# A four-layer graph network on one core: frames of counts that hold one tile each, the first block's panels moved to the end, block ends counted in groups, low one-hots against a PSUM iota, and a wait moved into a loop

## The chip, the core and the metric

The kernel runs on one core of a Trainium2 chip. The metric is the device time of one execution, in microseconds (us); before the change it is 7200.89 us, the median of three runs (7191.73 to 7232.2). One execution was recorded by the profiler.

## The reference

There are 12,500 nodes with 64 features and 200,000 edges sorted by their destination `dst`; each edge has 32 attributes and one of 16 types. Four layers follow one another, each of the form `x = x + layer(relu(layernorm(x)))`:

```python
x = x + L0(h)   # segment_sum((h @ weight[type])[src], dst) + bias + h @ loop_weight
x = x + L1(h)   # concat(h, segment_sum(h[src], dst)) @ W.T + b
x = x + L2(h)   # mean over dst of mlp(concat(h[src], h[dst], attr)) + h @ Wn + bn
x = x + L3(h)   # concat(h, segment_sum(concat(h[src], attr) @ W1 + b1, dst)) @ W2 + b2
```

`src` is drawn evenly over all nodes. `dst` is drawn as 12500 u squared, so that the first nodes have many edges each and the last ones few.

## The kernel before

**Units of work.** 128 edges are a tile, 4 tiles (512 edges) a group; there are 392 groups. 128 nodes are a window (98 of them), 7 windows a block of nodes (14 blocks). The kernel runs setup, `first_nodes` (a table of projected features), and then `layer_phase` for layers 0 to 3. Groups 0 to 383 of layer 0 and groups 272 to 383 of layers 1 and 3 are written out one by one (the static part). Behind them `run` does the last 8 groups and the last block in a loop with lengths read from a table (the dynamic part). Layer 2 is a loop throughout.

**A group, the gathered way.** GpSimd gathers the rows of the 512 sources by 4 indirect DMAs (line 1128) into one of 8 `msg` buffers. VectorE compares the edges' destinations with `window_iota` into `sel` (line 1514), TensorE multiplies and sums them (line 1811), and VectorE adds the result to `acc`, the sums of all nodes (line 1531).

**Counts.** The sums over the sources of the first 272 groups need no gather in layers 1 and 3. Layer 0 builds a table for them: for a frame (a few neighbouring destinations) it counts how many edges go from each of the 12,544 sources to each destination of the frame. A frame's width is the most destinations that its tiles may span. `PANEL_SHAPES` lists (groups, tiles to a frame, width); before, the first 192 groups have frames of two tiles, the other 80 frames of one tile, 704 frames and 20 panels in all. For a pair of tiles VectorE makes one-hots of the source's low 7 bits (`low_hot`, line 1559) and of its high part with the destination (`frame_hot`, line 1570). TensorE multiplies them unit by unit into two PSUM tensors (`count_pair`, line 1835), ScalarE casts each unit into `frames` (`evacuate`, line 1348), SyncE stores a group's frames to `counts` (line 1220), and VectorE checks one window of them (`certify`, line 1587). This work is spread over the 384 steps of layer 0 by `pairs_before`, one step to a gathered group, in proportion to width + 3. In a step TensorE does `sum_up` and then the step's pairs; ScalarE places the next group's attributes and then evacuates; VectorE selects the next group, certifies, makes the one-hots and adds the sums.

**Panels.** In layers 1 and 3 a panel is a run of groups whose frames fill up to 512 columns. TensorE multiplies the 98 windows of node features with the panel's counts (line 1851), in 4 pieces of 25, 25, 25 and 23 matmuls; SyncE loads the pieces into a ring of 3. That is one step to a piece, 80 steps. When a panel is complete, ScalarE copies its low half (line 1449), VectorE adds the halves (`combine`, line 1594), and in the next four steps `add_frames` adds each frame to its place in `acc`, one instruction to a frame (line 1613):

```python
if (t - begin) % LOADED == 0:
    count = min(LOADED, end - t)
    _, bases = nc.values_load_multi_w_load_instructions(
        frame_base[0:1, bass.ds(frames_before[k] + t, count)], engines=[DVE_ENGINE], ...
to = acc[0:D, bass.ds(bases[(t - begin) % LOADED], fw)]
```

The destinations' first columns are thus read into registers, up to 16 at a time, by line 1607. `panel_sums` and `panel_ps` have two buffers each. The gathered groups 272 to 383 are spread over the same steps.

**Blocks.** When all sums of a block are there, the five parts of `node_part` finish its nodes, one part to a step: ScalarE copies `acc` to `stage` (line 1364), TensorE multiplies it (line 1872), VectorE adds to `xs` (line 1629), normalises, and so on. `BLOCK_ENDS` gives, in steps of 8 groups, the group by which a block is complete; `part_at` is made from it at build time, on all engines alike. In layers 1 and 3 four blocks come behind the last panel: 5, 12, 6 and 7. VectorE then copies the iota back (line 1746), waits for the last static block's store (line 1748), and goes into `run`.

`ordered` is 1 where the inputs keep the bounds of the static part, and 0 sends everything to the dynamic part in many passes.

## Time and profile before

| what | value |
|---|---|
| median of three runs | 7200.89 us (7191.73 to 7232.2) |
| the profiled execution's own time | 7163.53 us |
| its span | 7161.7 us |
| mean granted TensorE clock | 0.743 of full speed |
| setup and `first_nodes` | 0 to 240 us |
| layer 0 | 240 to 2717 us |
| layer 1 | 2717 to 3638 us |
| layer 2 | 3638 to 6342 us |
| layer 3 | 6342 to 7162 us |

PE is TensorE's matmuls, PEld its weight loads, DVE VectorE, ACT ScalarE, POOL GpSimd, SPq SyncE's DMA issues. Reads into registers are not counted as busy: on VectorE they are seen as idle time with the releaser "issue", and in the chain of waits as "DVEq".

### The profile page before, as it was taken

To read this page: it belongs to the slowest core of one execution; us is meant where nothing else is said; L and a number is where in the kernel's file an instruction comes from. 1 tells how busy PE (TensorE), PEld (TensorE's weight loads), DVE (VectorE), ACT (ScalarE), POOL (GpSimd) and SP (SyncE) were. 2 spreads that over 40 slices of the span, in tenths; PEclk is the share of its full clock that TensorE was granted. 3 is DMA by queue.
4 is the path that set the end of the run, shared out by engine and by line. 5 is a ranking of instruction groups with operands and counts; after the bars stand their busy time and mean duration, and the time that the engine had idled before them with its cause. 6 is when DMAs were issued, how large, how long until landed. Compare 5 with 4: busy or idle time off the path is not lost. (4 is left out here: it accounts for less than half of the span.)

```text
span 7161.7 us, 86379 instructions
## 1 busy us (share of the span) xinstructions
PE 4714.0 (66%) x24800; PEld 3020.3 (42%) x24815; DVE 2438.5 (34%) x6392; ACT 2060.6 (29%) x3761; POOL 3998.2 (56%) x4125
## 2 busy tenths in 40 slices
PE   6565665666676656888646666666666666668885
PEld 3343443333333332344435554455545555533433
DVE  6443343333443333434222222222222222234232
ACT  5333333333566550010112222222222222210000
POOL 0466666666666555655246665555555555546653
PEclk8656567677666677888667887777777777778886
DMA  5433333332333335655222222222222222245562
GB/s 212 148 70 71 73 77 77 78 80 76 103 105 110 99 98 178 210 199 199 66 54 63 64 64 60 61 62 60 59 59 58 60 59 58 60 144 203 191 206 74
DMA packets 626790, 724.54 MB, mean 101 GB/s; under 512 B 235557, under 2 KB 526858, under 8 KB 607084
## 3 DMA queue, kind: packets, MB, share of 16 engines
q1 hardware_dynamic: 427578, 506.86, 21.5%
q0 software_dynamic: 130976, 185.66, 11.7%
q10 hardware_dynamic: 67986, 28.96, 1.5%
q8 instruction: 123, 2.02, 0.1%
q14 instruction: 127, 1.04, 0.0%
HBM read 518.59 MB, written 201.58 MB: 101 GB/s over the span
## 5 line engine op out<-in xcount | busy, mean ns | idle before, releaser
L1117 POOL DMA_INDIRECT layer_msg<-snd_table,layer_idx x1565 | 1480.3, 946 | 1305.7 <-DMA rel_table<-first_rows 442.8
L1128 POOL DMA_INDIRECT layer_msg<-rel_table,idx_rel x1536 | 1556.7, 1013 | 840.0 <-issue 420.9
L1811 PE MATMUL layer_sum_ps<-layer_sel,layer_msg 128*128 128x128 f32 (+14 forms) x8192 | 1139.7, 292 | 986.3 <-issue 445.8
L1835 PE MATMUL layer_unit_ps<-layer_frame_hot,layer_low_hot 128*128 128x350 bf16 (+9 forms) x3792 | 1111.5, 440 | 758.9 <-ACT layer_frames L1348 425.6
L1811 PEld LDWEIGHTS layer_sum_ps<-layer_sel,layer_msg 128*97 128x97 f32 (+2 forms) x8192 | 1069.4, 209 | 1161.1 <-issue 638.6
L1348 ACT CAST layer_frames<-layer_unit_ps 128x700 fp8e4<-128x700 f32 (+9 forms) x1268 | 953.1, 785 | 1341.0 <-remote 539.0
L1128 POOL DMA_INDIRECT layer_msg<-h_table,idx_src x896 | 849.9, 949 | 658.5 <-issue 238.5
L1851 PE MATMUL layer_panel_ps<-layer_piece,layer_pairs 128*128 128x504 fp8e4 (+9 forms) x3920 | 953.8, 399 | 124.6 <-issue 84.5
L1835 PEld LDWEIGHTS layer_unit_ps<-layer_frame_hot,layer_low_hot 128*128 128x128 bf16 x3792 | 395.3, 124 | 1310.4 <-issue 614.0
L1522 DVE TENSOR_TENSOR layer_msg<-layer_pre_ps,layer_msg 128x512 f32<-128x512 f32 x392 | 270.3, 690 | 1128.6 <-remote 696.0
L1851 PEld LDWEIGHTS layer_panel_ps<-layer_piece,layer_pairs 128*128 128x128 f16 x3920 | 391.2, 103 | 622.1 <-issue 253.5
L1531 DVE TENSOR_TENSOR acc<-acc,layer_sum_ps 64x64 f32 (+15 forms) x632 | 130.3, 206 | 1418.2 <-DMA rel_table<-first_rows 649.3
L1794 PEld LDWEIGHTS layer_pre_ps<-layer_rcv,layer_sel_t 128*128 128x128 f32 x3144 | 489.0, 221 | 266.9 <-issue 266.9
L1318 ACT COPY layer_attr_t<-layer_flip_ps 128x128 f32<-128x128 f32 x394 | 104.9, 266 | 1677.8 <-remote 1178.0
L1570 DVE TENSOR_SCALAR layer_frame_hot<-count_iota,frame_key 128x588 bf16<-128x588 f16 (+9 forms) x1088 | 560.7, 563 | 58.3 <-remote 35.3
L1791 PE MATMUL layer_pre_ps<-w_edge,layer_attr_t 128*128 128x512 f32 x786 | 531.1, 766 | 0.0
L1794 PE MATMUL layer_pre_ps<-layer_rcv,layer_sel_t 128*128 128x128 f32 x3144 | 472.8, 300 | 0.0
L1613 DVE SCALAR_TENSOR_TENSOR acc<-layer_panel_sums,ordered,acc 64x14 f32 (+9 forms) x1408 | 319.6, 227 | 444.2 <-issue 259.0
L1514 DVE TENSOR_TENSOR layer_sel_bf<-rel_dst,layer_window_iota 128x512 bf16<-128x512 f32 x395 | 269.9, 684 | 385.3 <-DMA rel_table<-first_rows 172.9
L1449 ACT COPY layer_low_sums<-layer_panel_ps 64x504 f32<-64x504 f32 (+9 forms) x40 | 22.0, 551 | 951.0 <-PE layer_panel_ps L1851 366.8
L1514 DVE TENSOR_TENSOR layer_sel<-rel_dst,layer_window_iota 128x256 f16<-128x256 f32 (+15 forms) x632 | 229.5, 370 | 128.6 <-issue 57.0
L1328 ACT ACTIVATE layer_msg<-layer_msg 128x512 f32<-128x512 f32 x392 | 251.1, 641 | 50.8 <-DVE layer_msg L1522 36.9
(236 smaller groups left out, 3780.6 us busy)
## 6 DMA issues: line engine op xcount, KB each, us to landing
layer_piece<-counts SPq DMA_DIRECT2D x48, 1575.0 KB
layer_attr<-in_edge_attr_dram SPq DMA_DIRECT2D x790, 64.0 KB
rel_table<-first_rows SPq DMA_DIRECT2D x98, 512.0 KB, 2.7
layer_piece<-counts SPq DMA_DIRECT2D x24, 1500.0 KB
layer_piece<-counts SPq DMA_DIRECT2D x16, 1593.8 KB
layer_rcv<-rcv_table SPq DMA_DIRECT2D x396, 64.0 KB
layer_msg<-snd_table,layer_idx POOLq DMA_INDIRECT x1565
layer_piece<-counts SPq DMA_DIRECT2D x16, 1543.8 KB
```

Of the source, the lines that this page charges most:

```text
L1117: nc.gpsimd.indirect_dma_start(msg[g][:, u, 0:2 * D if dense else width], None, of, bass.IndirectOffsetOnAxis(ap=idx_slot[g][:, u:u + 1], ...
L1128: nc.gpsimd.indirect_dma_start(msg[g][:, u, 0:2 * D if dense else width], None, of, bass.IndirectOffsetOnAxis(ap=idx[:, at:at + 1], axis=0 ...
L1348: nc.scalar.copy(part, of, saturate=False).then_inc(evacuated, 1)
L1514: nc.vector.tensor_tensor(to[:, :, 0:span], rel.unsqueeze(2).to_broadcast([P, TILES, span]), window_iota[:, 0:span].unsqueeze(1).to_broadc ...
L1522: nc.vector.tensor_tensor(rows_of, pre_ps[g % 2][:, :], rows_of, ALU.add).then_inc(pre_added, 1)
L1570: last = nc.vector.tensor_scalar(frame_hot[j][:, v, 0:HI * fw], count_iota[:, 0:HI * fw], frame_key[:, tile:tile + 1], None, ALU.is_equal)
L1613: nc.vector.scalar_tensor_tensor(out=to, in0=panel_sums[k % 2][:, t * fw:(t + 1) * fw], scalar=ordered[0:D, 0:1], in1=to, op0=ALU.mult, op ...
L1791: nc.tensor.matmul(pre_ps[g % 2][:, :], attr_t[g % 2][:, :], w_edge[:, :], start=True, stop=False)
L1794: last = nc.tensor.matmul(pre_ps[g % 2][:, u * H:(u + 1) * H], sel_t[g % 2][:, u * P:(u + 1) * P], rcv[j][:, :], start=False, stop=u == TI ...
L1811: last = nc.tensor.matmul(sum_ps[g % 2][0:sums, 0:span], msg[g][:, u, c0:c1], sel[j][:, u, 0:span], start=n_part == 0, stop=n_part == len( ...
L1835: last = nc.tensor.matmul(unit_ps[unit % 2][:, half * 512:half * 512 + cols], low_hot[k % HOT][:, 2 * (r % 2) + v, :], frame_hot[j][:, v, ...
L1851: last = nc.tensor.matmul(panel_ps[k % 2][:, 0:count * fw].rearrange("p (t f) -> p t f", t=count), pairs[:, w // KW, (w % KW) * 2 * D:(w % ...
```

## The change

`PANEL_SHAPES` has 22 panels, all with one tile to a frame: 1088 frames where there were 704, with widths 4 to 17. `SEQUENCE` gives the order in which layers 1 and 3 take the panels: 3 to 21, then 0, 1 and 2 (78 groups, all within block 0). Those three have 128, 100 and 84 frames; the first two of the new order have 64 each. There are 88 steps in place of 80. Block 0 is now finished last, and three blocks come behind the last panel's combining: 7, 12 and 0. `BLOCK_ENDS` is counted in single groups, so that a block of layer 0 can begin up to 7 steps earlier; the last static block of layer 0 begins at step 379 and not behind the last group. `low_hot` is made against `window_iota`, which lies in PSUM, and not against `iota` in SBUF. The wait for `stored` moves from ahead of `run` into `nodes`, behind the 8 groups of the loop. `FRAME_MAX` falls from 20 to 17, the most frames' columns that a one-hot buffer must hold.

```diff
-PANEL_SHAPES = ((42, 2, 6), (28, 2, 9), (22, 2, 11), (19, 2, 13), (18, 2, 14), (15, 2, 17), (15, 2, 17),
-                (13, 2, 19), (12, 2, 20), (8, 2, 20), (9, 1, 13), (9, 1, 13), (9, 1, 14), (9, 1, 14), (9, 1, 14),
-                (8, 1, 15), (8, 1, 15), (8, 1, 16), (6, 1, 17), (5, 1, 17))
+PANEL_SHAPES = ((32, 1, 4), (25, 1, 5), (21, 1, 6), (16, 1, 8), (16, 1, 8), (14, 1, 9), (13, 1, 9),
+                (12, 1, 10), (11, 1, 11), (11, 1, 11), (10, 1, 12), (10, 1, 12), (9, 1, 13), (9, 1, 13),
+                (9, 1, 14), (9, 1, 14), (9, 1, 14), (8, 1, 15), (8, 1, 15), (8, 1, 16), (7, 1, 17),
+                (5, 1, 17))
...
-FRAME_MAX = 20
+FRAME_MAX = 17
...
-BLOCK_ENDS = (14, 19, 23, 27, 30, 33, 35, 38, 40, 42, 44, 46, 48, 49)
+BLOCK_ENDS = (107, 151, 184, 212, 237, 259, 279, 298, 316, 333, 349, 364, 379)
...
+LATE = 3
+SEQUENCE = list(range(LATE, len(PANELS))) + list(range(LATE))
+LATE_GROUPS = PANELS[LATE][0]
...
-            first_step[b] = (BLOCK_ENDS[b] - FIRST) * PER
+            first_step[b] = BLOCK_ENDS[b] - FIRST * PER
...
-                ends = min(BLOCK_ENDS[b] * PER, DENSE_1)
-                ready = PIECES * (2 + min(k for k, panel in enumerate(PANELS) if panel[0] + panel[1] >= ends))
+                ends = min(BLOCK_ENDS[b], DENSE_1)
+                needed = [k for k, n in enumerate(SEQUENCE) if PANELS[n][0] < ends and (b == 0 or n >= LATE)]
+                ready = PIECES * (2 + max(needed))
...
-            for _, ng, tiles, _, _ in PANELS:
+            for n in SEQUENCE:
+                _, ng, tiles, _, _ = PANELS[n]
...
-                            iota[:, :].unsqueeze(1).to_broadcast([P, TILES, P]), ALU.is_equal)
+                            window_iota.unsqueeze(1).to_broadcast([P, TILES, P]), ALU.is_equal)
...
 def add_frames(k, s):
-                    _, _, _, fw, _ = PANELS[k]
+                    g0, _, tiles, fw, _ = PANELS[SEQUENCE[k]]
+                    at = g0 * TILES // tiles if tiles == 2 else g0 * TILES - DOUBLE_1 * TILES // 2
...
-                                frame_base[0:1, bass.ds(frames_before[k] + t, count)], engines=[DVE_ENGINE],
+                                frame_base[0:1, bass.ds(at + t, count)], engines=[DVE_ENGINE],
...
                 def nodes(b, m):
+                    dve.wait_ge(stored, 16 * stores * (static_blocks + 1))
...
-                    dve.wait_ge(stored, 16 * stores * (static_blocks + 1))
                 run(dve, DVE_ENGINE, edges, nodes, next_window)
```

The other lines of the diff put `PANELS[SEQUENCE[k]]` for `PANELS[k]` on each engine, and let setup's bounds say that the first 78 groups lie in block 0.

## Rows read from the trace of the kernel before

**Rows 1.** Windows by stage: us, busy (instructions) of PE, PEld, DVE, ACT, POOL; clock; DMA.

```profile
240.00:2717.00 2477.00, 1547.47 (x7420) 912.54 (x7420) 991.03 (x2597) 1062.17 (x1730) 1589.47 (x1571) 0.65 0.33 84
2717.00:3638.00 921.00, 677.47 (x3606) 356.85 (x3606) 335.59 (x1152) 78.06 (x174) 454.59 (x479) 0.81 0.50 166
...
6342.00:7162.00 820.00, 608.93 (x3172) 292.35 (x3172) 260.12 (x981) 36.84 (x48) 452.68 (x479) 0.81 0.53 175
```

**Rows 2.** The page's costliest groups: count, busy us, mean ns, idle before.

```profile
L1128 POOL DMA_INDIRECT layer_msg<-rel_table,idx_rel x1536 | 1556.7, 1013 | 840.0 <-issue 420.9
...
L1835 PE MATMUL layer_unit_ps<-layer_frame_hot,layer_low_hot 128*128 128x350 bf16 (+9 forms) x3792 | 1111.5, 440 | 758.9 <-ACT layer_frames L1348 425.6
...
L1128 POOL DMA_INDIRECT layer_msg<-h_table,idx_src x896 | 849.9, 949 | 658.5 <-issue 238.5
```

**Rows 3.** Windows in layer 0; POOL's instructions there are the gathers of line 1128.

```profile
400.00:1700.00 1300.00, 806.74 (x4026) 504.35 (x4027) 510.59 (x1416) 471.63 (x776) 881.10 (x875) 0.65 0.32 75
1800.00:2600.00 800.00, 544.29 (x2423) 282.68 (x2423) 322.76 (x785) 479.38 (x768) 488.20 (x476) 0.66 0.37 105
```

**Rows 4.** Groups by shape, layer 0.

```profile
L1559 DVE TENSOR_TENSOR layer_low_hot<-low_key,iota 128x512 bf16<-128x512 f32 x272 | 186.1, 684 | 0.0
...
L1348 ACT CAST layer_frames<-layer_unit_ps 128x1000 fp8e4<-128x1000 f32 x80 | 78.1, 993 | 139.0 <-PE layer_unit_ps L1835 70.8 <-remote 55.5 <-DVE layer_cert L1587 6.6
...
L1570 DVE TENSOR_SCALAR layer_frame_hot<-count_iota,frame_key 128x588 bf16<-128x588 f16 x168 | 55.5, 378 | 43.8 <-remote 27.6 <-PE layer_unit_ps L1835 9.1 <-issue 6.8
L1570 DVE TENSOR_SCALAR layer_frame_hot<-count_iota,frame_key 128x1960 bf16<-128x1960 f16 x80 | 54.9, 728 | 0.0
...
L1348 ACT CAST layer_frames<-layer_unit_ps 128x550 fp8e4<-128x550 f32 x88 | 53.8, 619 | 112.2 <-remote 54.9 <-PE layer_unit_ps L1835 39.5 <-issue 9.2
...
L1514 DVE TENSOR_TENSOR layer_sel<-rel_dst,layer_window_iota 128x512 f32<-128x512 f32 x8 | 5.5, 683 | 7.4 <-issue 4.9 <-PE layer_sum_ps L1811 2.5
```

**Rows 5.** Waits in 1800 to 2600 us: who for whom, us, times, longest.

```profile
PEld layer_unit_ps L1835 <- ACT layer_frames L1348: 287.8, 292, 5.5
...
POOL layer_msg L1128 <- PE layer_sum_ps L1811: 148.5, 42, 9.0
```

**Rows 6.** Timeline of VectorE in layer 3's first panel: start, us; idle before in brackets.

```profile
6436.90 5.57 DVE L1613 SCALAR_TENSOR_TENSOR acc<-layer_panel_sums,ordered,acc 64x6 f32 x16 [3.80 <-issue]
6443.60 1.61 DVE L1613 SCALAR_TENSOR_TENSOR acc<-layer_panel_sums,ordered,acc 64x6 f32 x5 [1.13 <-issue]
```

**Rows 7.** Windows cut where a panel's sums are combined (line 1594), layers 1 and 3.

```profile
2777.00:2829.70 52.70, 37.63 (x171) 14.36 (x169) 21.60 (x96) 0.58 (x1) 31.84 (x34) 0.84 0.57 195
2829.70:2862.70 33.00, 28.04 (x146) 11.87 (x146) 15.85 (x71) 0.56 (x1) 19.43 (x21) 0.90 0.57 198
2862.70:2890.70 28.00, 26.06 (x138) 11.14 (x138) 12.84 (x56) 0.57 (x1) 18.41 (x20) 0.94 0.68 247
2890.70:3481.60 590.90, 476.33 (x2696) 248.52 (x2696) 227.43 (x812) 51.76 (x115) 336.19 (x353) 0.88 0.56 189
...
6519.00:7080.60 561.60, 446.73 (x2422) 215.75 (x2420) 179.44 (x705) 25.34 (x34) 337.42 (x357) 0.86 0.56 188
```

**Rows 8.** Chain of waits, 6400 to 6480 us, by line.

```profile
by line: DVE acc L1613 31.5%; DVEq L1607 24.8%; issue 19.2%; PE layer_panel_ps L1851 11.4%; DVEq L1613 6.4%; DVE layer_sel L1514 2.3%; DVE acc L1531 1.8%; ACT layer_low_sums L1449 0.7%; DVEq L1076 0.6%; PE layer_sum_ps L1811 0.5%; another c
```

**Rows 9.** Timeline of VectorE, end of layer 1.

```profile
3518.04 0.68 DVE L1629 SCALAR_TENSOR_TENSOR xs<-layer_post_ps,ordered,xs 128x448 f32<-128x448 f32 x1
...
3541.53 0.68 DVE L1629 SCALAR_TENSOR_TENSOR xs<-layer_post_ps,ordered,xs 128x448 f32<-128x448 f32 x1
...
3577.46 0.29 DVE L1746 COPY layer_window_iota<-iota 128x128 f32<-128x128 f32 x1 [0.22 <-DVE xs L1629]
3592.31 0.69 DVE L1514 TENSOR_TENSOR layer_sel<-rel_dst,layer_window_iota 128x512 f16<-128x512 f32 x1 [14.55 <-issue]
```

**Rows 10.** Line 1746, the end of each static part, and who waited.

```profile
L1746 DVE COPY layer_window_iota<-iota x3: 294/295/296, 2671.9 to 7129.5; 128x128 f32<-128x128 f32 x3
...
  DVE layer_sel L1514: 4.6, 1
```

More of the change, by code:

```diff
@@ L389, in _ @@
                 link(nc.vector.tensor_scalar(double[:, :], group_of[:, :], float(DOUBLE_1), None, ALU.is_lt))
-                count_from(lowest, BLOCK_ENDS[0] * PER, 1.0)
-                for end in BLOCK_ENDS[1:NB - 1]:
-                    count_from(lowest, end * PER)
+                count_from(lowest, BLOCK_ENDS[0], 1.0)
+                for end in BLOCK_ENDS[1:]:
+                    count_from(lowest, end)
                 link(nc.vector.tensor_scalar(lowest[:, :], lowest[:, :], float(BLK), None, ALU.mult))
                 count_from(outside, DENSE_1, float(N))
-                link(nc.vector.tensor_scalar(highest[:, :], outside[:, :], float(8 * BLK - P), None, ALU.add))
+                link(nc.vector.tensor_scalar(width_step[:, :], group_of[:, :], float(LATE_GROUPS),
+                                             float(BLK - 8 * BLK), ALU.is_lt, ALU.mult))
+                link(nc.vector.scalar_tensor_tensor(out=highest[:, :], in0=outside[:, :],
+                                                    scalar=float(8 * BLK - P), in1=width_step[:, :], op0=ALU.add,
+                                                    op1=ALU.add))
                 link(nc.vector.memset(any_bad[:, :], 0.0))
@@ L874, in layer_phase @@
             if b <= 7:
-                ends = min(BLOCK_ENDS[b] * PER, DENSE_1)
-                ready = PIECES * (2 + min(k for k, panel in enumerate(PANELS) if panel[0] + panel[1] >= ends))
-            if BLOCK_ENDS[b] * PER > DENSE_1:
+                ends = min(BLOCK_ENDS[b], DENSE_1)
+                needed = [k for k, n in enumerate(SEQUENCE) if PANELS[n][0] < ends and (b == 0 or n >= LATE)]
+                ready = PIECES * (2 + max(needed))
+            if BLOCK_ENDS[b] > DENSE_1:
                 ready = max(ready, 1 + min(z for z in range(STEPS)
-                                           if DENSE_1 + groups_by[z] >= BLOCK_ENDS[b] * PER))
+                                           if DENSE_1 + groups_by[z] >= BLOCK_ENDS[b]))
             first_step[b] = ready
@@ L1224, in load_piece @@
                 def load_piece(s):
-                    _, ng, tiles, fw, at = PANELS[s // PIECES]
+                    _, ng, tiles, fw, at = PANELS[SEQUENCE[s // PIECES]]
                     w = ng * TILES // tiles * PIECE * fw
@@ L1443, in _ @@
                         if z % PIECES == 0 and 0 <= k < len(PANELS):
-                            _, ng, tiles, fw, _ = PANELS[k]
+                            _, ng, tiles, fw, _ = PANELS[SEQUENCE[k]]
                             cols = ng * TILES // tiles * fw
@@ L1589, in combine @@
                 def combine(k):
-                    _, ng, tiles, fw, _ = PANELS[k]
+                    _, ng, tiles, fw, _ = PANELS[SEQUENCE[k]]
                     cols = ng * TILES // tiles * fw
@@ L1841, in multiply_piece @@
                 def multiply_piece(k, s):
-                    _, ng, tiles, fw, _ = PANELS[k]
+                    _, ng, tiles, fw, _ = PANELS[SEQUENCE[k]]
                     count = ng * TILES // tiles
```

## The prediction

> **What bounds the kernel now.** I first cut the span by stage [rows 1]. No engine fills a stage: in layer 0 GpSimd is busy 1589 of 2477 us and TensorE 1547, in layer 1 TensorE 677 of 921. So I looked at each stage for the wait that ends last. Layer 2 holds no line of the diff, and setup only a few small ones; they stand at no change.
>
> Layer 0 goes at the pace of its steps, one gathered group (4 gathers) to a step. Two windows [rows 3] give it: 875 gathers in 1300 us are 218.75 groups, 5.94 us each, while the frames hold two tiles; 476 in 800 us are 119 groups, 6.72 us each, while they hold one. A gather takes 1013 ns and some 0.27 to 0.30 us of issue lie behind it (840 us of idle for 1536 gathers, half of it "issue" [rows 2]; the rest comes with blocks and waits), so gathers alone would allow about 5.2 us. They don't set the pace: GpSimd itself waits for TensorE to free a `msg` buffer, 42 times for 148.5 us, and TensorE's count matmuls wait for ScalarE's casts, 287.8 us out of 800 [rows 5]. The loop between TensorE and ScalarE sets it, in the late part above all: there ScalarE is busy 479.4/119 = 4.03 us a step and TensorE 544.3/119 = 4.57, against 2.16 and 3.69 in the early one [rows 3].
>
> The static parts of layers 1 and 3 go panel by panel. The windows between combines [rows 7] show two kinds. The first three panels' frames (84, 56, 44) are added in 52.7, 33.0 and 28.0 us. The next 16 panels take 590.9/16 = 36.9 us each in layer 1, blocks and gathered groups included, and 561.6/16 = 35.1 in layer 3. In the first, VectorE is "busy" 21.6 of 52.7 us and yet is the bound: the chain over such a stretch lies on line 1613 with 31.5% and on the register reads of line 1607 with 24.8%, TensorE's panels with 11.4% [rows 8]. The timeline [rows 6] gives a price to a frame: 16 adds in 5.57 us behind 3.80 us of reads, 5 in 1.61 behind 1.13, so 21 frames in 12.11 us, 0.577 us a frame. 84 frames: 48.4 us, and the window is 52.7, 4.3 us more. Thus D(n) = 0.577 n + 4.3 us; for 56 it says 36.6 where 33.0 was measured, so it may be 10% high there. It exceeds TensorE's 36.9 us from about 56 frames on.
>
> **Dense layers.** Frames rise from 704 to 1088 and panels from 20 to 22, panel matmuls from 1960 to 2156. VectorE, alone, would pay 384 x 0.577 = 222 us a layer, but the panels with few frames hide theirs behind TensorE. In the new order (64, 64, 56, 52 and on down to 20, then 128, 100, 84) the first two and the last three are bound by VectorE.
>
> Layer 1 before: first combine 2777.0 to line 1746 at 3577.5 [rows 7, 9], 800.5 us. After: 2 x D(64) = 82.4. Then 17 panels: the 16 of before, 590.9, and one more like the third window, 28.0, in which TensorE is busy 26.06; but the 112 gathered groups now go over 88 steps, not 80, so 17 panels hold 86.5 and not 16 + 1 windows' 89.6 + 5.6, 8.7 fewer. That window has 146 matmuls, 98 of them the panel's; the other 48 for 5.6 groups at 26.06/146 us make 1.5 us a group, minus 13. So 606. Then D(128) + D(100) = 78.2 + 62.0 = 140.2. In these late panels block 6 begins as well; a block behind the adds costs 23.5 us here, by 3518.04 to 3541.53 [rows 9], and in a stretch bound by VectorE I count it in full. Behind the last combine come the 84 frames, 52.7, with block 7 beside them, and then blocks 12 and 0, 47.0. Sum 952, +151.
>
> Layer 3: 1746 at 7129.5 [rows 10], first combine three windows like those of layer 1 before 6519.0, at 6405: 724.5 us. After: 82.4 + (561.6 + 26.5 - 13 = 575) + 140.2 + one block + 52.7 + two blocks. The stretch behind the last combine was 48.9 us for four blocks, 12.2 each; so 12.2 and 24.4. Sum 887, +162. Together +313 us. The orders of block 0 and of the table cost no more by themselves. The 12.5% more bytes of counts (118.8 to 133.7 MB by the shapes, stored once and loaded twice) run at 189 to 247 GB/s and a DMA share of 0.56 to 0.68 [rows 7], under matmuls or adds that take longer; with that cover gone, 14.9 MB at 247 GB/s would be 60 us a layer.
>
> Bounds of the dense term. Below: if the reads ahead of the adds overlapped more, a frame would cost near 0.35 us, the adds' own cadence (5.57/16), and the two layers would lose about 100 us, from two more panels and 128 frames at 45 us. Above: block parts and gathered sums interleave badly with the long adds; 360 us.
>
> **Layer 0, the counts.** By the shapes, units go from 1268 to 1580, matmuls from 3792 to 3160 and their columns from 1,427,600 to 1,065,600; ScalarE's cast columns rise from 947,200 to 1,065,600. Casts take 993 ns for 1000 columns and 619 ns for 550 [rows 4], so 0.165 us + 0.83 ns a column: 312 x 0.165 + 118,400 x 0.00083 = 150 us more. VectorE's `frame_hot` goes by 728 ns for 1960 and 378 for 588 [rows 4], 0.255 ns a column, of which 354,760 go: 90 us less, not on the path. The three memsets where the width drops go with them, under 4 us.
>
> What this does depends on how it is spread. Pairs go to steps by width + 3. Before, the 80 one-tile groups have 1407 of 4385 weights, the last 123 of 384 steps; after, the same widths have 1427 of 3480, 157 steps. A late step so has 22% less of counts: ScalarE's 4.03 us falls by 0.85. As the wait is for ScalarE, the 6.72 should fall by nearly that; I take 5.95. In the early 227 steps TensorE's count columns go from 960,800/261 = 3680 a step to 2610, ScalarE's from 1840 to 2610 (+0.64 us and a unit's fixed part, to some 2.9 us). TensorE's 3.69 falls to about 2.9. The two become equal; I take 5.70, a small gain. Before 261 x 5.94 + 123 x 6.72 = 2377; after 227 x 5.70 + 157 x 5.95 = 2228: -149. The last static block no longer stands behind the last group: a block costs some 12 us, as in the four behind the last combine of layer 3 (48.9 us). Earlier blocks merely move. In all -160. Bounds: 0 (the longer ScalarE takes all) and -365 (5.2 us a step, less the blocks' own delays). TensorE's granted clock is 0.65 of full speed in both windows [rows 3], 0.84 to 0.94 in the dense ones [rows 7], a share of time between its levels of 1.2 and 2.4 GHz. I leave it there; were it 0.60 after, TensorE's 2.9 to 3.6 us a step would be 0.25 to 0.3 longer, up to 110 us over 384 steps, within the bound of 0.
>
> **Low one-hots from PSUM.** The 272 instructions took 684 ns with both inputs in SBUF; the comparison of the same shape that reads `window_iota` in PSUM took 683 [rows 4]. Nothing; the bounds are +-0.1 us x 272, hidden on VectorE either way.
>
> The gathers take 1013 ns in layer 0 and 949 without counts beside them [rows 2], 64 ns x 1536 = 98 us of GpSimd. That could be the one-hots' doing; since GpSimd waits for TensorE, none of it reaches the end in my sum. The Trainium skill ("SBUF — State Buffer", section "Who interferes with whom") has VectorE and GpSimd share one pair of SBUF ports under an exclusive lock, and a VectorE instruction with an input in PSUM doesn't take it; by that rule 272 x 0.68 us of lock go, up to 98 us of gathers. The trace shows the excess, not its cause; my sum would be the same by either, and the rule only lowers the floor of the first rival.
>
> **The moved wait.** Behind line 1746 the next selection in layer 1 begins after 14.55 us, in layer 0 after 4.6 [rows 9, 10]: the last static block's store. Moved behind the loop's groups it is over when reached, -10 us; layer 3's block ends in little to store, layer 0 has its own wait small: -1.5. Queued behind the old place were VectorE's selections and all that follows; behind the new one only the last block's parts. -11.5, bounds 0 and -20.
>
> **Sum.** 7163.5 (own time of the profiled execution) + 313 - 160 - 11.5 = 7305, a ratio of 1.0197. The median of the three runs is 7200.9, 0.5% above that execution; times the ratio, 7343, say 7340 us.
>
> **Rivals.**
> (A) Layer 0 drops to the gathers' floor. For it: GpSimd's issue and gathers need only 5.2 us, TensorE loses 25% of its columns, and a waiting chain can release more than its busy time. Against: ScalarE's work rises, and blocks stall the step anyway. It decides if a step falls below 5.3 us. -340 in place of -160: 7125, 7162 on the median. This is the one that ends on the other side.
> (B) The frames are cheap or hidden. For it: 56 frames took 33.0, less than D says, and a short read was 1.13 us for 5. Against: the chain [rows 8]. It decides if a 128-frame panel takes under 50 us. +100 in place of +313: 7092, 7129 on the median.
> (C) Layer 0 gains nothing: ScalarE, already the releaser [rows 5], has 150 us more. 7465, 7503 on the median.
> (D) The change does not do what it says: a tile wider than its new bound sets `ordered` to 0 and costs many passes, far above all here. The tile spans of dst as 12500 u squared lie within the widths, so 1%.
>
> **How the numbers follow.** Mine 0.58, A 0.14, B 0.11, C 0.16, D 0.01. Mine has its own range, 7240 to 7430, from +313 by -60 and +50 and -160 by -50 and +60. To leave out no more than 2 in 10 the range takes in A and half of C: 7140 to 7490. A measurement of this kernel tells 0.5% from no change, 7165 to 7237. Faster: B, most of A, 0.16. Same: the edge of mine and the rest of A, 0.11. Slower: 0.73.
>
> **What would show it.** In the profile after: line 1613 x2176 and a larger share of line 1607 in the chain; the last two distances between combines near 78 and 62 us with TensorE busy under half; 17 near 35.6; steps of layer 0 near 5.7 and 5.95 us, casts near 1210 us busy; `low_hot` still 684 ns; the selection behind 1746 within 5 us in layer 1. The prediction is wrong if the adds of a step run without their reads in between (B), if layer 0's step reaches 5.2 (A), or if its late step stays at 6.7 (C).

## The result and the profile after

The changed kernel took 7290.77 us, the median of four runs (7273.74 to 7305.39), against 7196.31 us (7176.05 to 7232.2) for the kernel before on the same chip: a ratio of 1.0142, interval 1.0116 to 1.0169. It is slower, as forecast, by 94 us where 139 were forecast.

The experiments ran later, on chips numbered 2 (e1 to e8), 9 (e9 to e11) and 15 (e12). The kernel before takes 5720 to 5729 us on each of the three, so they are taken together here and called the second chip. The same change costs more there: 5915.09 us, 1.0341 (1.0324 to 1.0359). The first measurement has no chip number. "The first chip" is a name for it; whether it was a slower chip or a slower time of one isn't known. All ratios are to the kernel before, measured beside the run on the same chip, and all traces of experiments are of the second.

The page after, first chip, its costliest groups; they answer to [rows 2]:

```profile
L1141 POOL DMA_INDIRECT layer_msg<-rel_table,idx_rel x1536 | 1497.2, 975 | 895.0 <-issue 409.1
...
L1849 PE MATMUL layer_unit_ps<-layer_frame_hot,layer_low_hot 128*128 128x300 bf16 (+10 forms) x3160 | 1015.0, 452 | 791.7 <-ACT layer_frames L1361 488.6
L1361 ACT CAST layer_frames<-layer_unit_ps 128x600 fp8e4<-128x600 f32 (+10 forms) x1580 | 1082.2, 724 | 1206.9 <-PE layer_unit_ps L1849 568.6
...
L1627 DVE SCALAR_TENSOR_TENSOR acc<-layer_panel_sums,ordered,acc 64x8 f32 (+12 forms) x2176 | 485.2, 223 | 626.3 <-issue 341.3
```

The count matmuls lost a quarter of their columns and only 9% of their time: 1111.5 to 1015.0 us, 440 to 452 ns each although they are narrower. (The nanoseconds are a mean over instructions that overlap one another.) Windows of layer 0 show a lower clock beside it (all of the layer, then the two stretches of [rows 3]; the clock is the third number from the end):

```profile
240.00:2660.00 2420.00, 1496.24 (x6687) 857.56 (x6687) 877.55 (x2551) 1186.80 (x2035) 1523.38 (x1563) 0.56 0.36 91
400.00:1700.00 1300.00, 819.47 (x3575) 470.45 (x3576) 463.75 (x1485) 638.39 (x1101) 829.30 (x853) 0.52 0.36 91
1800.00:2600.00 800.00, 507.33 (x2269) 283.07 (x2269) 285.66 (x711) 416.65 (x672) 491.12 (x501) 0.63 0.35 96
```

The granted clock, a mean between the levels of 1.2 and 2.4 GHz, fell from 0.65 of full speed [rows 1] to 0.56. Most of the fall is early: 0.65 to 0.52 in the first stretch, 0.66 to 0.63 in the second. A step takes 1300/(853/4) = 6.10 us in the first stretch, 5.94 before, and 800/(501/4) = 6.39 in the second, 6.72 before.

A combine is VectorE's adding of a panel's two halves (line 1594 before, 1607 after), and its start marks a finished panel. The copy is that of the iota at the end of a static part (line 1746 before, 1761 after). The windows of the dense layers 1 and 3, cut at combines (first two panels of layer 1, the next 17, the two before the last combine, the rest to the copy; then the last three of layer 3), answer to [rows 7]:

```profile
2767.70:2833.40 65.70, 56.29 (x282) 23.05 (x281) 34.24 (x151) 1.16 (x2) 40.56 (x43) 0.90 0.67 234
2833.40:3420.00 586.60, 497.79 (x2751) 251.54 (x2750) 256.26 (x957) 48.95 (x108) 326.98 (x344) 0.90 0.62 207
3420.00:3484.70 64.70, 48.71 (x216) 22.31 (x214) 37.21 (x154) 5.37 (x12) 25.89 (x29) 0.84 0.53 180
3484.70:3544.40 59.70, 33.70 (x150) 18.76 (x150) 24.95 (x112) 4.59 (x10) 16.83 (x18) 0.70 0.20 39
3544.40:3637.50 93.10, 33.79 (x122) 25.80 (x123) 37.02 (x126) 10.86 (x25) 0.00 (x0) 0.54 0.07 20
7074.10:7132.40 58.30, 43.71 (x189) 17.91 (x187) 31.85 (x140) 2.42 (x3) 26.27 (x28) 0.83 0.55 188
7132.40:7189.40 57.00, 30.37 (x123) 13.80 (x123) 24.41 (x111) 2.32 (x3) 15.23 (x17) 0.68 0.13 12
7189.40:7255.60 66.20, 13.21 (x36) 8.47 (x36) 21.08 (x91) 3.69 (x4) 0.00 (x0) 0.50 0.03 7
```

The span of each trace can be cut at five instructions of VectorE, the three copies and the first combine of layers 1 and 3:

| stretch, us | first chip, before | after | forecast | second chip, before (e10) | after (e9) |
|---|---|---|---|---|---|
| start to copy in layer 0 | 2671.9 | 2660.0 (-11.9) | -160 | 2305.3 | 2214.9 (-90.4) |
| to first combine, layer 1 | 105.1 | 107.7 (+2.6) | 0 | 84.3 | 102.2 (+17.9) |
| to copy, layer 1 | 800.4 | 869.8 (+69.4) | +151 | 639.3 | 776.2 (+136.9) |
| to first combine, layer 3 | 2827.5 | 2819.2 (-8.3) | -10 | 2099.7 | 2084.4 (-15.3) |
| to copy, layer 3 | 724.5 | 798.9 (+74.4) | +162 | 570.2 | 704.1 (+133.9) |
| to the end | 32.2 | 31.4 (-0.8) | -1.5 | 31.7 | 30.4 (-1.3) |
| span | 7161.7 | 7287.0 (+125.3) | +141 | 5730.5 | 5912.2 (+181.7) |

On the first chip each column is one execution. The one before took 7163.5 us, 33 less than its median, and the one after 7288.8, 2 less than its own. So the parts add up to 125 us where the medians differ by 94, and a part of 12 us can't be told from nothing there.

Two terms of the forecast were too large, with opposite signs: the dense layers cost +144 and not +313, layer 0 gave 12 and not 160.

### The profile page after: what moved, and what is told of

It is laid out like the page before. It is cut to its first block and busy times, and to the rows that moved or that the text cites. A ratio compares the mean times of both kernels' runs of the same rounds, so it can differ in the third digit from the quotient of the medians.

```text
span 7287.0 us, 87827 instructions
## 1 busy us (share of the span) xinstructions
PE 4777.0 (66%) x24560; PEld 3005.1 (41%) x24575; DVE 2508.5 (34%) x7162; ACT 2190.8 (30%) x4076; POOL 3931.8 (54%) x4125
## 3 DMA queue, kind: packets, MB, share of 16 engines
q0 software_dynamic: 130976, 185.66, 11.9%
## 5 line engine op out<-in xcount | busy, mean ns | idle before, releaser
L1141 POOL DMA_INDIRECT layer_msg<-rel_table,idx_rel x1536 | 1497.2, 975 | 895.0 <-issue 409.1
L1825 PE MATMUL layer_sum_ps<-layer_sel,layer_msg 128*128 128x128 f32 (+14 forms) x8192 | 1204.9, 303 | 939.7 <-ACT layer_msg L1341 560.3
L1825 PEld LDWEIGHTS layer_sum_ps<-layer_sel,layer_msg 128*97 128x97 f32 (+2 forms) x8192 | 1140.0, 222 | 1116.7 <-DVE layer_hidden_acc L1544 561.4
L1849 PE MATMUL layer_unit_ps<-layer_frame_hot,layer_low_hot 128*128 128x300 bf16 (+10 forms) x3160 | 1015.0, 452 | 791.7 <-ACT layer_frames L1361 488.6
L1361 ACT CAST layer_frames<-layer_unit_ps 128x600 fp8e4<-128x600 f32 (+10 forms) x1580 | 1082.2, 724 | 1206.9 <-PE layer_unit_ps L1849 568.6
L1865 PE MATMUL layer_panel_ps<-layer_piece,layer_pairs 128*128 128x504 fp8e4 (+7 forms) x4312 | 1072.6, 404 | 139.2 <-issue 98.9
L1849 PEld LDWEIGHTS layer_unit_ps<-layer_frame_hot,layer_low_hot 128*128 128x128 bf16 x3160 | 289.5, 125 | 1346.5 <-issue 621.1
L1865 PEld LDWEIGHTS layer_panel_ps<-layer_piece,layer_pairs 128*128 128x128 f16 x4312 | 427.6, 102 | 711.9 <-issue 309.6
L1627 DVE SCALAR_TENSOR_TENSOR acc<-layer_panel_sums,ordered,acc 64x8 f32 (+12 forms) x2176 | 485.2, 223 | 626.3 <-issue 341.3
L1583 DVE TENSOR_SCALAR layer_frame_hot<-count_iota,frame_key 128x392 bf16<-128x392 f16 (+12 forms) x1088 | 468.4, 477 | 59.0 <-PE layer_unit_ps L1849 41.3
```

Source lines behind the costliest of these rows:

```text
L1141: nc.gpsimd.indirect_dma_start(msg[g][:, u, 0:2 * D if dense else width], None, of, bass.IndirectOffsetOnAxis(ap=idx[:, at:at + 1], axis=0 ...
L1361: nc.scalar.copy(part, of, saturate=False).then_inc(evacuated, 1)
L1583: last = nc.vector.tensor_scalar(frame_hot[j][:, v, 0:HI * fw], count_iota[:, 0:HI * fw], frame_key[:, tile:tile + 1], None, ALU.is_equal)
L1627: nc.vector.scalar_tensor_tensor(out=to, in0=panel_sums[k % 2][:, t * fw:(t + 1) * fw], scalar=ordered[0:D, 0:1], in1=to, op0=ALU.mult, op ...
L1825: last = nc.tensor.matmul(sum_ps[g % 2][0:sums, 0:span], msg[g][:, u, c0:c1], sel[j][:, u, 0:span], start=n_part == 0, stop=n_part == len( ...
L1849: last = nc.tensor.matmul(unit_ps[unit % 2][:, half * 512:half * 512 + cols], low_hot[k % HOT][:, 2 * (r % 2) + v, :], frame_hot[j][:, v, ...
```

## The experiments

**What a read into registers costs (e1, e2).** The timeline of VectorE, changed kernel, first chip, in the 128-frame panel and then in the 100-frame panel:

```profile
3423.00 5.46 DVE L1627 SCALAR_TENSOR_TENSOR acc<-layer_panel_sums,ordered,acc 64x4 f32 x16 [1.49 <-issue]
3429.51 5.41 DVE L1627 SCALAR_TENSOR_TENSOR acc<-layer_panel_sums,ordered,acc 64x4 f32 x16 [1.06 <-issue]
...
3501.18 1.95 DVE L1627 SCALAR_TENSOR_TENSOR acc<-layer_panel_sums,ordered,acc 64x5 f32 x6 [3.80 <-issue]
```

All three runs of adds stand behind a read of 16 destinations. The first two reads took 1.10 us, the third 3.62. The forecast's price came from a read of the second kind [rows 6]. Sorted over all 200 reads of the changed kernel (medians), those whose first index is a multiple of four take 0.60 us for 8 values, 0.85 for 12 and 1.10 for 16, and 0.22 to 0.27 us more for each value over a multiple of four; the others take 1.19 for 5, 2.07 for 9, 3.18 for 14 and 3.60 for 16, whether the index is one, two or three places off. That is 0.25 us for four values against 0.22 for one. Two kernels test whether the index is the cause.

```diff
 # e1_align
-                    return (frames_before[k + 1] - frames_before[k]) * s // PIECES
+                    return (frames_before[k + 1] - frames_before[k]) // 4 * s // PIECES * 4
 # e2_reads_off
-                        if (t - begin) % LOADED == 0:
-                            count = min(LOADED, end - t)
+                        if t == begin or (t - begin - 1) % LOADED == 0:
+                            count, first = 1 if t == begin else min(LOADED, end - t), t
...
-                        to = acc[0:D, bass.ds(bases[(t - begin) % LOADED], fw)]
+                        to = acc[0:D, bass.ds(bases[t - first], fw)]
```

> The changed kernel, but each of a panel's four steps begins at a frame whose number is a multiple of four. In the trace of the changed kernel a read of 16 destinations into registers takes 1.10 us where its first value's index is a multiple of 4, and 3.60 us elsewhere. Theory (the index sets the price of a read): every read of 16 takes about 1.1 us, the reads of a layer fall from some 178 to under 100 us, the last two distances between combines from 64.7 and 59.7 to about 53 and 50 us, and the whole is 45 to 80 us shorter, a ratio of 1.004 to 1.008 to the kernel before. Rival (the long reads come from traffic on the chip at that moment): as many reads over 3 us as now, 1.014 as the changed kernel.

> The changed kernel, but a step's first destination is read alone, and the others behind it in runs of up to 16 that begin one place off a multiple of four; the reads in all are as many values as before. Theory (index): nearly all reads of 15 and 16 take 3.4 to 3.6 us, the 128-frame panel takes some 20 us more, the two 64-frame panels 10 each, 60 to 120 us in all, a ratio of 1.022 to 1.031. Rival (traffic): only one more short read a step, 0.35 us, of which the panels bound by VectorE show 4 to 8 us a layer, 1.015 to 1.017.

e1 took 5815.17 us, 1.0159 (1.0142 to 1.0176); the changed kernel there takes 1.0341, so 100 us less, more than expected. e2 took 6029.25 us, 1.0535 (1.0517 to 1.0553), 114 us more. The reads of the two dense layers add up to 328 us in e9, 160 in e1 and 491 in e2, and those over 3 us number 19, none and 46. The first adds of layer 1 in e2, and in the changed kernel on the same chip (e9):

```profile
2319.32 0.22 DVE L1627 SCALAR_TENSOR_TENSOR acc<-layer_panel_sums,ordered,acc 64x8 f32 x1 [0.53 <-DVE acc L1544]
2323.28 5.12 DVE L1627 SCALAR_TENSOR_TENSOR acc<-layer_panel_sums,ordered,acc 64x8 f32 x15 [3.73 <-issue]
```

```profile
2327.31 5.64 DVE L1627 SCALAR_TENSOR_TENSOR acc<-layer_panel_sums,ordered,acc 64x8 f32 x16 [1.28 <-issue]
```

The read in front of the long run begins one place further on, brings one value less and yet costs 2.45 us more. Not all of e2's 114 us is the index's: its 176 further reads, of one value each at 0.31 us, are 55 of the 163 us by which its reads grew. e1 has no such addition. Single reads are longer than their kind, up to 5.65 us for 16 values in e2, so traffic may add to one now and then. As the cause of the two kinds it is refuted, and the index is shown. The Trainium skill ("Runtime: NRT & Kernel Launch", section "Instruction fetch mechanics") gives about 200 ns a register, in bulk too; the runs agree for a start off a multiple of four (0.22 us) and not for a start on one (0.07 us). The late panels: 128 frames take 65.5 us in e1 and 65.4 in e9, since their steps of 32 were already aligned (the expectation, about 53, had overlooked that); 100 frames fall from 59.4 to 46.3.

**Which part carries the loss (e3, e4, e9, e10).**

```diff
 # e3_old_shapes: in the changed kernel
-PANEL_SHAPES = ((32, 1, 4), (25, 1, 5), ... (5, 1, 17))
+PANEL_SHAPES = ((42, 2, 6), (28, 2, 9), ... (5, 1, 17))
-FRAME_MAX = 17
+FRAME_MAX = 20
 # e4_first_order: in the changed kernel
-LATE = 3
+LATE = 0
```

> The changed kernel with the panel shapes of the kernel before (704 frames, 20 panels); order, block ends, low one-hots and the moved wait as changed. Theory (the shapes carry nearly all of the +94 us): the clock of layer 0 is back at 0.65, layer 1's static part near 800 us, and the whole within 0.5% of before, rather 10 to 20 us faster by the moved wait. Rival (order of panels or block ends carry a part): 1.004 or more.

> The changed kernel with the panels in their natural order, 0 to 21: the 128-, 100- and 84-frame panels come first and four blocks come behind the last panel. Theory (the order is nearly neutral: the adds of the three large panels are exposed at either end, and one block more stands at the end, 23 us in layer 1 and 12 in layer 3): 1.013 to 1.020. Rival (putting them last is what costs, as TensorE has nothing left to run ahead with): 1.005 or less.

> The changed kernel as it is, once more, beside the kernel before on the chip of the experiments, where the kernel before takes 5722 to 5726 us. The runs e1 to e8 fell on a chip that is a fifth faster than that of the first measurement, and the unchanged changed kernel has not run there. Theory (on this chip layer 0 goes at the pace of the gathers and the clock is high, so the dense layers' frames are less hidden): 1.033 to 1.036, as e4, e6 and e8 say, about 5920 us. Rival (the ratio of the first measurement holds on any chip): 1.012 to 1.017.

> The kernel before, for its trace on the chip of the experiments. Theory: a step of layer 0 takes about 5.3 us, 1.02 gather by 4 and 0.305 us between them, so layer 0's static part ends near 2310 us; the changed kernel's ends at 2217, half of it by the shapes (the old shapes with the other edits ended at 2263) and half by the low one-hots (with them from SBUF it ended at 2261). The dense layers are as with the old shapes, 739 and 603 us from the copy before to the copy behind them. Rival (the old shapes' run gained elsewhere too): an end of layer 0 under 2280.

e3 took 5718.74 us, 0.9989 (0.998 to 0.9999); e4 5918.77 us, 1.0337 (1.032 to 1.0354); e9 5915.09 us, 1.0341; e10, the kernel before as a kernel of its own, 1.0004. The shapes so carry the whole loss: 196 us lie between e9 and e3, 195 between e9 and the kernel before. Aligned reads take 100 us of it back (e1), but they give 41 us with the old shapes too (e3 to e11 below). Aligned on both sides, the new shapes still cost 138 us (5677 in e11, 5815 in e1). That part goes with the adds, 384 more a layer, and wasn't split further. e4's ratio is above what was expected, as all are on this chip, but the order is neutral, as its theory had it. e9's rival fell: the ratio isn't the same on any chip. e10's layer 0 ended at 2305.3, as expected, and its dense stretches were shorter than e3's: 639.3 and 570.2 us against 649.2 and 602.6, 42 us in all. e11 and e12 below, with the same 704 frames, differ in the order of the panels alone, and by 42 us too. So with 704 frames the new order costs about what the low one-hots give; with 1088 frames it costs nothing (e4). The block ends counted in groups had no run of their own.

**What sets the pace of layer 0 (e5, e6, e7).**

```diff
 # e5_filled: in count_pair, in steps with no part of a block in them or in the four before
+                        if fill:
+                            nc.tensor.matmul(post_ps[:, 0:256], low_hot[k % HOT][:, 2 * (r % 2), :],
+                                             frame_hot[j][:, 0, 0:256], start=True, stop=True)
 # e6_half_cast: frames set to 0 once, then
-                        nc.scalar.copy(part, of, saturate=False).then_inc(evacuated, 1)
+                        nc.scalar.copy(part[:, 0:1], of[:, 0:1], saturate=False).then_inc(evacuated, 1)
 # e7_iota_back
-                            window_iota.unsqueeze(1).to_broadcast([P, TILES, P]), ALU.is_equal)
+                            iota[:, :].unsqueeze(1).to_broadcast([P, TILES, P]), ALU.is_equal)
```

> The changed kernel; in the steps of layer 0 away from a block's parts TensorE does one matmul of 256 columns more ahead of each unit's wait, into a PSUM bank that is idle there; its product is never read. Some 1200 of them. Theory (the count matmuls lost their gain to a lower clock: 0.56 granted over layer 0 where it was 0.65): the granted clock of layer 0 rises to 0.65 or above, and layer 0 takes no longer than 2420 us, perhaps 50 to 100 less. Rival (the clock doesn't matter, the rows of units do): 1200 x 0.11 to 0.21 us of added work shows, layer 0 gets 100 to 250 us longer.

> The changed kernel; ScalarE casts only half of the columns of each unit in layer 0, and the counts of the other half stay 0, so sums of layers 1 and 3 lack them. Casts fall from some 0.69 to 0.43 us each, 400 us in all. Theory (ScalarE and TensorE share the pace, TensorE at its low clock is nearly full with 3.9 us of matmuls and 2.2 of weights a step): layer 0 falls by 50 to 150 us. Rival (ScalarE alone sets the pace): 250 us or more. Second rival (GpSimd's gathers set it): nothing.

> The changed kernel with the low one-hots made against the iota in SBUF again. In the trace of the changed kernel the gathers of layer 0 take 975 ns, 1013 before. Theory: the gathers go back to about 1010 ns, 55 us more of GpSimd's busy time, and the whole changes by under 15 us (1.012 to 1.017), since GpSimd waits for free buffers. Rival (the gathers set the pace of layer 0): +50 us, 1.021.

e6 leaves out half of the counts, so its sums are wrong and only its time is of use. Windows over 240 to 2200 us on the second chip: the kernel before (e10), the changed (e9), e5, e6.

```profile
240.00:2200.00 1960.00, 1390.46 (x6947) 801.08 (x6947) 929.16 (x2438) 976.45 (x1613) 1509.29 (x1479) 0.72 0.39 98
```

```profile
240.00:2200.00 1960.00, 1408.89 (x6634) 790.57 (x6634) 875.12 (x2531) 1157.54 (x2023) 1493.61 (x1531) 0.61 0.42 112
```

```profile
240.00:2200.00 1960.00, 1425.27 (x7781) 858.61 (x7782) 877.59 (x2532) 1172.81 (x2023) 1494.35 (x1529) 0.72 0.42 112
```

```profile
240.00:2200.00 1960.00, 1400.43 (x6614) 802.24 (x6615) 876.32 (x2532) 773.12 (x2017) 1496.43 (x1522) 0.61 0.42 111
```

Here too the change lowers the clock, 0.72 to 0.61; with the old shapes it is 0.73 (e3). But that costs nothing here. e5 lifts it back to 0.72 with some 1150 more matmuls, which also brings the count matmuls from a mean of 429 ns to 392; e6 takes 384 us from ScalarE. Layer 0 ends at 2211.7 and 2219.7, against 2214.9 in e9 (ratios 1.0335 and 1.0334): neither the 50 to 100 us that e5 might have won nor its rival's loss. GpSimd does 1531 gathers in 1960 us, 5.12 us a step, which is four times the 0.976 us of a gather and the 0.305 us between two. Not one of the 1535 intervals between layer 0's gathers is over 0.6 us, in e9 or in e10: GpSimd is never held up, and the gathers set the pace on this chip, e6's second rival. e7 shows it from the other side. Its gathers, then those of e10 and e9:

```profile
L1141 POOL DMA_INDIRECT layer_msg<-rel_table,idx_rel x1536 | 1550.2, 1009 | 487.3 <-issue 461.2
```

```profile
L1128 POOL DMA_INDIRECT layer_msg<-rel_table,idx_rel x1536 | 1566.6, 1020 | 486.9 <-issue 463.8
```

```profile
L1141 POOL DMA_INDIRECT layer_msg<-rel_table,idx_rel x1536 | 1499.0, 976 | 487.1 <-issue 459.9
```

With the one-hots from SBUF the gathers go from 976 back to 1009 ns, 51 us in all, and layer 0 ends 46 us later, at 2261.1: 5961.21 us, 1.0406 (1.0389 to 1.0423). The one-hots themselves take 683 ns from SBUF and 679 from PSUM. The expectation, under 15 us of change, was wrong here, its rival's 50 us right.

**The wait (e8).**

```diff
+                    dve.wait_ge(stored, 16 * stores * (static_blocks + 1))
                 run(dve, DVE_ENGINE, edges, nodes, next_window)
```

> The changed kernel with the wait for the last static block's store ahead of the loop again. Theory: the selection behind the copy of the iota begins 14 us after it in layer 1 and not 5, the whole 8 to 12 us longer, a ratio of 1.0155, near the edge of what is told apart. Rival (something else of the loop's start is late anyway): no change.

5928.16 us, 1.0354 (1.0338 to 1.037), an interval that overlaps e9's. The end of layer 1 in VectorE's timeline, e8 and then e9:

```profile
3099.04 0.29 DVE L1760 COPY layer_window_iota<-iota 128x128 f32<-128x128 f32 x1 [0.22 <-DVE xs L1643]
3113.92 0.69 DVE L1527 TENSOR_TENSOR layer_sel<-rel_dst,layer_window_iota 128x512 f16<-128x512 f32 x1 [14.59 <-issue]
```

```profile
3093.29 0.29 DVE L1761 COPY layer_window_iota<-iota 128x128 f32<-128x128 f32 x1 [0.22 <-DVE xs L1643]
3098.19 0.69 DVE L1527 TENSOR_TENSOR layer_sel<-rel_dst,layer_window_iota 128x512 f16<-128x512 f32 x1 [4.61 <-issue]
```

The wait is there and costs 10 us at its place. From this copy to layer 3's first combine e8 takes 2088.9 us and e9 2084.4, so some 5 us of it is seen later, and behind layer 3's copy 33.1 against 30.4. In total e8 lies 13 us above e9 and 9 above e4 and e6, which have the moved wait too. That points to the 8 to 12 us expected, but the intervals overlap.

**A faster version (e11, e12).** Old shapes, aligned steps, everything else as changed; e12 with the natural order too.

```diff
 # e11_old_shapes_align: e3 and, with n the panel's frames and `at` as in add_frames
-                    return (frames_before[k + 1] - frames_before[k]) * s // PIECES
+                    return n if s == PIECES else max(0, (at + n * s // PIECES) // 4 * 4 - at)
 # e12_best: e11 and
-LATE = 3
+LATE = 0
```

> The changed kernel with the old panel shapes and with steps that begin at a destination whose index is a multiple of four. Theory (index sets the price of a read, frames are exposed in the 84- and 56-frame panels and partly in others): 15 to 25 us a layer less than the old shapes alone (0.9989), a ratio of 0.990 to 0.994, faster than both kernels. Rival (with 704 frames the reads are hidden): 0.998.

> The kernel of e11 (old panel shapes, aligned steps, low one-hots from PSUM, block ends by groups, moved wait) with the panels in their natural order. Theory: with 704 frames the order of the change costs, since from first combine to the copy e3 took 649 and 603 us in layers 1 and 3, and the kernel before 639 and 570; taken back it gives 30 to 45 us: 5632 to 5647 us, a ratio of 0.984 to 0.987. Rival (e3's block ends or its wait carry that difference, not the order): 0.992 as e11.

e11 took 5677.26 us, 0.9925 (0.9908 to 0.9942), e12 5635.01 us, 0.984 (0.9824 to 0.9857), both as expected. In e11 the reads fall from 252 us (e3) to 115, and the dense stretches to 624.7 and 580.9 us; in e12 these are 599.5 and 556.7. e12 beats both kernels, the one before by 94 us.

## Why the prediction came out right, and where it did not

The median lies in the forecast's own range, 7240 to 7430 us, and the direction is right for the reason given, adds that TensorE doesn't cover. The size is right by luck, as both large terms were too large.

**The dense layers, +313 forecast, +144 measured.** The step that failed is "0.577 us a frame". It is 0.35 us for the add, as said, and between 0.07 and 0.24 for the read, by the index, and both reads of the row that set the price were of the dear kind. The steps of the new 64- and 128-frame panels begin at multiples of four, so the panels that the argument rested on were the ones with cheap reads. D(128) was to be 78.2 us and was 64.7 and 58.3; D(64) 41.2 and was 33.2 and 32.4 in layer 1, 38.3 and 30.7 in layer 3, near what TensorE needs anyway; D(100), whose reads are mostly dear, 62.0 and was 59.7 and 57.0. Priced read by read, the old 84-frame panel is 29.4 us of adds, 16.1 of reads and 7.2 left over, and D(64), D(128) and D(100) come out at 34.0, 60.8 and 61.2 us, within 4.4 of every one measured. By this estimate the price accounts for 33 us a layer, 65 of the 169 by which the term was too large.

The rest has other places. In layer 1 the parts are -17 us for the first two panels against the forecast (65.7 for 82.4), -19 for the next 17 (586.6 for 606), -39 for the two late ones with block 6 in them (124.4 for 140.2 + 23.5) and -7 behind the last combine (93.1 for 99.7). In layer 3 they are -13, -27, -37 and -11. The two late panels alone are 122.0 us by the estimate above, so the block in them, counted in full, cost next to nothing: it went beside the adds. The mechanism held, that VectorE, its register reads among it, bounds the panels with many frames: TensorE is busy 33.7 of 59.7 us in the 100-frame panel, and on the second chip the late panels take 65.4 and 59.4 us, as on the first, while those bound by TensorE take 24 to 34 us in place of 24 to 44. That is the likely reason why the change costs more there, +271 us for the two layers: TensorE's faster panels cover fewer adds. No run varied TensorE's pace alone.

**Layer 0, -160 forecast, -12 measured.** The step that failed is "As the wait is for ScalarE, the 6.72 should fall by nearly that", and the 5.70 beside it. On the first chip a late step fell to 6.39, not 5.95, and an early one rose to 6.10. ScalarE did get lighter late, from 4.03 to 3.33 us a step, so its load wasn't what set the step one for one. Early, "TensorE's 3.69 falls to about 2.9" failed: it is busy 3.95 us a step (819.47 us over 853/4 steps), with fewer columns and the clock at 0.52. The clock's fall was named as a risk of up to 110 us and not put in the sum. Fewer columns went with a lower clock on both chips, and on the second one e5's idle-time matmuls brought it back, so the work itself moves it. That the clock is what took the gain on the first chip is argued from [rows 1, 3] and the windows after, not shown: no experiment ran there. What the traces do show is where the gathers' own gain went. The gathers of layer 0 before (240 to 2717 us), then after (240 to 2660 us), first chip:

```profile
L1128 POOL DMA_INDIRECT layer_msg<-rel_table,idx_rel x1535 | 1555.5, 1013 | 821.4 <-issue 420.9 <-PE layer_sum_ps L1811 225.2 <-DMA rel_table<-first_rows 175.3
```

```profile
L1141 POOL DMA_INDIRECT layer_msg<-rel_table,idx_rel x1535 | 1496.1, 975 | 876.0 <-issue 409.1 <-PE layer_sum_ps L1825 299.8 <-DMA rel_table<-first_rows 167.1
```

They are 59 us shorter, and GpSimd waits 75 us longer for TensorE to free a buffer. The block behind the last group, counted at 12 us, gave 5 to 6.5: from the end of the last gather to layer 1's first combine there are 161.1 us before and 156.1 after on the first chip, and 118.1 and 111.6, 6.5 less, on the second.

Of the sizes, the casts rose by 129 us (953.1 to 1082.2), 150 forecast, and `frame_hot` fell by 92, 90 forecast. The sign "casts near 1210 us busy" gave what is ScalarE's whole busy time, 1186.8, and not the casts'.

TensorE is held on the first chip in another way as well. Layer 1's first panel, the kernel before, first chip and then second (e10); the trace shows no wait for either:

```profile
2742.42 0.40 PE L1851 MATMUL layer_panel_ps<-layer_piece,layer_pairs 128*128 128x504 fp8e4 x1 [1.00 <-issue]
2743.85 0.40 PE L1851 MATMUL layer_panel_ps<-layer_piece,layer_pairs 128*128 128x504 fp8e4 x1 [1.03 <-issue]
...
2747.35 0.58 PE L1851 MATMUL layer_panel_ps<-layer_piece,layer_pairs 128*128 128x504 fp8e4 x1 [1.64 <-issue]
2748.77 0.58 PE L1851 MATMUL layer_panel_ps<-layer_piece,layer_pairs 128*128 128x504 fp8e4 x1 [0.85 <-issue]
```

```profile
2369.99 6.20 PE L1851 MATMUL layer_panel_ps<-layer_piece,layer_pairs 128*128 128x504 fp8e4 x25
```

25 matmuls follow one another in 6.20 us on the second chip; on the first they stand a microsecond apart. What holds them is not in the trace and stays open.

**Rival A** (the gathers' floor) is the state of the second chip, but already of the kernel before there: 5.30 us a step (1479 gathers in the window above), 5.12 after. So up to the last gather, which ended at 2271.5 us and now at 2205.5, layer 0 gained what the gathers became shorter (67.6 us) and nothing by a release of waits; the other 24 us lie between the last gather and the copy. Cut by edits, 46 of the 90 us go with the one-hots (e7 to e9) and 48 with the shapes (e3's copy at 2262.8, e9's at 2214.9; e3's gathers took 994 ns, e9's 976; why the shapes shorten them isn't shown). 18 us come back behind the copy: the last static block now lies beside the last steps, the copy comes sooner, and the loop's groups then wait for their gathers, so that behind the last gather the net is the 6.5 us above. TensorE's timeline in e9, then in e10:

```profile
2232.25 2.02 PE L1825 MATMUL layer_sum_ps<-layer_sel,layer_msg 128*97 128x128 f32 x8 [3.51 <-DMA layer_msg<-rel_table,layer_idx]
2237.11 2.02 PE L1825 MATMUL layer_sum_ps<-layer_sel,layer_msg 128*97 128x128 f32 x8 [2.85 <-DMA layer_msg<-rel_table,layer_idx]
2242.38 2.02 PE L1825 MATMUL layer_sum_ps<-layer_sel,layer_msg 128*97 128x128 f32 x8 [3.25 <-DMA layer_msg<-rel_table,layer_idx]
2249.33 2.02 PE L1825 MATMUL layer_sum_ps<-layer_sel,layer_msg 128*97 128x128 f32 x8 [4.94 <-DMA layer_msg<-rel_table,layer_idx]
```

```profile
2318.16 1.98 PE L1811 MATMUL layer_sum_ps<-layer_sel,layer_msg 128*97 128x128 f32 x16 [0.57 <-DVE acc L1531]
2320.50 1.98 PE L1811 MATMUL layer_sum_ps<-layer_sel,layer_msg 128*97 128x128 f32 x16 [0.35 <-issue]
```

**Rival B** (cheap frames) had half of the truth: its +100 for the two layers lies nearer to 144 than 313 does, but a 128-frame panel stayed above its 50 us. **Rival C** (layer 0 gains nothing) gave the right size for layer 0. Whether ScalarE is its cause stays open: a lighter ScalarE (e6) was tried only on the second chip, where the gathers set the pace anyway, and on the first the late step didn't stay at its 6.7.

**Low one-hots from PSUM, 0 forecast.** Right for the instruction (684 before [rows 4], 679 ns after). The effect on the gathers was seen in [rows 2] and taken as hidden; on the first chip it fell from 1013 to 975 ns, and whether any of it reached the end there isn't shown. On the second it gave 46 us. The rule of the Trainium skill that was weighed ("SBUF — State Buffer", section "Who interferes with whom") is that a VectorE instruction with at most one input in SBUF, outside the modes that use both ports, doesn't contend with GpSimd. The runs agree with its direction: of the 62 to 68 ns by which layer 0's gathers were longer than those of layers 1 and 3, about half (33 ns) went with the one input. Where the other half comes from isn't shown.

**The moved wait, -11.5 forecast.** On the first chip the next selection in layer 1 now begins 4.61 us after the copy where it was 14.55 [rows 9], and the whole stretch behind the copy is 8.3 us shorter. That is right in size at its place; e8's total points the same way and can't confirm it.

**Bytes of the table, 0 forecast.** Nothing in the runs speaks against it: panels of the middle take 34.5 us each (586.6/17) with 207 GB/s.

## What to carry to other kernels

Before a stall is given a price per item, sort all its instances by what their operands have in common (here the first index of a register read), since one row of it can be the exception. A sum whose large terms have opposite signs can be right by luck, so read the parts of a result, not only its total. Work taken from an engine that waits in a loop with others needn't shorten the loop; ask first which of them would be the floor, here the gathers.

## What the runs showed of the hardware

- A read of 16 values into VectorE's registers took 1.10 us from an index that is a multiple of four and 3.60 us from any other, on both chips; starting steps on such an index took 100 us off this kernel (e1).
- TensorE's granted clock over layer 0 fell when a quarter of the count columns went, 0.65 to 0.56 and 0.72 to 0.61, and rose from 0.61 to 0.72 when some 1150 matmuls of 256 columns were put in the idle time, with no change in the time where the gathers set the pace.
- One kernel took 7196 us in the first measurement and 5720 to 5729 on three chips later. The stretch that holds layer 2, where both kernels are the same, makes 728 of the 1476 us. TensorE's granted clock over the whole kernel is 0.743 in the slow case and 0.839 in the fast one, and in the slow case its matmuls at times stand apart with no wait in the trace.
- A VectorE comparison with one input in PSUM in place of two in SBUF left its own duration as it was and made GpSimd's gathers beside it 33 ns shorter.
